# Building the token list of an expert layer: five of six column groups on VectorE instead of every second, and six buffers instead of four

## The reference, cut to what matters

```python
x = x + mamba(layernorm(x), ...)
x = x + ffn(layernorm(x), ...)
# inside ffn, after attention; N = 16384 tokens, 8 experts, top 2, cap = 5120
probs = softmax(h @ router_weight)
top_p, top_i = top_k(probs, 2);  top_p = top_p / sum(top_p)
order = argsort(top_i.reshape(-1))            # choices, expert by expert
within = place of a choice in its expert;  keep = within < cap
padded_ids[slot of the choice] = its token;  padded_probs likewise
out = (gelu(tokens @ w1[e]) @ w2[e]) * padded_probs
moe = zeros.at[padded_ids].add(out)
```

## Time and profile before

| what | value |
|---|---|
| median of three executions | 6568.46 us |
| profiled execution, its own time | 6567.08 us |
| its span, first to last instruction | 6565.4 us |
| busy over the span | PE 93%, POOL 79%, DVE 64%, ACT 54% |
| stretch of the token list (first `hot_lane` to last matmul) | 4440.65 to 4610.45 us of the span |
| expert stage behind it | from 4616 us to the end |

### The profile page before, as it was taken

One profiled execution on the slowest core, in us unless ns is written; L12 is line 12 of the kernel. 1 busy time (PEld: TensorE's weight loads), 2 busy tenths in 40 slices (PEclk: granted clock), 3 DMA queues, 4 the chain that ended last, 5 costly groups with the idle time before them and its releaser, 6 DMA issues. The chain is left out here.

```text
span 6565.4 us, 78602 instructions
## 1 busy us (share of the span) xinstructions
PE 6120.1 (93%) x25316; PEld 3921.9 (60%) x25316; DVE 4215.0 (64%) x5430; ACT 3554.0 (54%) x6449; POOL 5192.8 (79%) x3956
## 2 busy tenths in 40 slices
PE   7999999999999999999998799965899999999999
PEld 3444444444444444444443688854788888888887
DVE  6999999999999999999999377774000000000000
ACT  6677676767776767676766588742222222222221
POOL 6999999999999999999999677739555555545454
PEclk9999999999999999999999999987999999999999
DMA  3555555555555555555555244340566666666554
GB/s 125 164 162 170 166 170 163 167 168 168 163 170 164 172 163 166 167 165 168 164 166 162 67 119 124 113 112 1 178 187 183 187 183 186 184 184 184 176 169 125
DMA packets 564794, 1029.82 MB, mean 157 GB/s; under 512 B 90722, under 2 KB 259172, under 8 KB 529824
## 3 DMA queue, kind: packets, MB, share of 16 engines
q1 hardware_dynamic: 457280, 669.05, 33.2%
q0 software_dynamic: 107104, 355.74, 18.2%
HBM read 926.31 MB, written 88.60 MB: 155 GB/s over the span
## 5 line engine op out<-in xcount | busy, mean ns | idle before, releaser
L365 POOL TENSOR_TENSOR m_dbu<-m_du,m_bb 128x1024 f32<-128x1024 f32 x1024 | 2394.3, 2371 | 0.0
L743 PE MATMUL m_y_bank<-m_prod,m_ident 128*128 128x512 f32 x4096 | 1977.2, 612 | 145.1 <-POOL m_prod L374 145.1
L516 ACT ACTIVATE m_decay<-m_delta,m_a_neg 128x512 f32<-128x512 f32 x2048 | 1419.8, 695 | 726.9 <-DVE m_h L626 724.9
L743 PEld LDWEIGHTS m_y_bank<-m_prod,m_ident 128*128 128x128 f32 x4096 | 789.4, 196 | 1124.5 <-issue 907.9
L626 DVE TENSOR_TENSOR_SCAN m_h<-m_decay,m_h_end,m_dbu 128x512 f32<-128x512 f32 x1024 | 1258.4, 1265 | 3.4 <-ACT m_decay L516 2.5
L1763 DVE TENSOR_SCALAR e_ye<-e_ybank,e_share 128x256 f32<-128x256 f32 x270 | 118.2, 479 | 1768.3 <-PE e_ybank L1796 1768.3
L626 DVE TENSOR_TENSOR_SCAN m_h<-m_decay,m_dbu 128x512 f32<-128x512 f32 x1024 | 1196.2, 1204 | 12.3 <-ACT m_decay L516 11.8
L1744 ACT ACTIVATE e_a<-e_ubank 128x512 f32<-128x512 f32 x540 | 322.4, 597 | 1473.8 <-PE e_ubank L1787 1473.8
L374 POOL TENSOR_TENSOR m_prod<-m_h,m_cb 128x1024 f32<-128x1024 f32 x416 | 985.9, 2370 | 20.4 <-issue 14.6
L1787 PE MATMUL e_ubank<-e_xT,s_w 128*128 128x256 f32 x4320 | 978.4, 380 | 1.3 <-ACT e_xT L1735 1.3
L1796 PE MATMUL e_ybank<-s_w,e_a 128*128 128x256 f32 x4320 | 954.5, 379 | 0.7 <-ACT e_a L1744 0.7
(11 more groups left out here) (211 smaller groups left out, 6683.8 us busy)
## 6 DMA issues: line engine op xcount, KB each, us to landing
m_bb<-rows_bc SPq DMA_DIRECT2D x1024, 256.0 KB, 3.8
m_cv<-rows_bc SPq DMA_DIRECT2D x608, 256.0 KB, 4.0
m_cb<-rows_bc SPq DMA_DIRECT2D x416, 256.0 KB, 3.4
m_xin<-in_x SPq DMA_DIRECT2D x32, 512.0 KB, 5.6
m_xres<-in_x SPq DMA_DIRECT2D x32, 512.0 KB, 5.4
x<-m_xres SPq DMA_DIRECT2D x32, 512.0 KB, 6.2
a_xa<-x SPq DMA_DIRECT2D x64, 256.0 KB, 2.9
a_xr<-x SPq DMA_DIRECT2D x64, 256.0 KB, 3.1
```

Source lines behind the costliest of these rows:

```text
L365: nc.gpsimd.tensor_tensor(dbu[:, slot], du[:, q[1], p * PC:(p + 1) * PC], bb[:, slot].unsqueeze(1).to_broadcast([P, PC, T]), ALU.mult).the ...
L516: nc.scalar.activation(decay[:, cc], delta[:, r, c], ACT.Exp, scale=a_neg[:, c, n:n + 1]).then_inc(decay_done, 1)
L743: ins = nc.tensor.matmul(y_bank[:, cc], ident[:], prod[:, slot, cc], start=False, stop=(n == NS - 1))
```

## The change

`BY_POOL` becomes every fifth group: 4, 9, 14, 19, 24 and 29, six groups in place of sixteen. VectorE makes the hot columns of 26 groups in place of 16. The ring of `hot_lane`, `hot_row` and `hot_column` has six buffers, so every wait on `placed` in the list reaches back six groups instead of four. Since `BY_POOL[-2]` is now group 24, the weights of block 0 are issued behind group 24 and no longer behind group 29, and those of block 1 behind group 29 and no longer behind 31.

```diff
@@ -1396,8 +1396,8 @@
     SPAN = 4
     EACH = SPAN * TOPK
     GROUPS = TILES // SPAN
-    HOT_RING = 4
-    BY_POOL = [g for g in range(GROUPS) if g % 2]
+    HOT_RING = 6
+    BY_POOL = [g for g in range(GROUPS) if g % 5 == 4]
     BY_VECTOR = [g for g in range(GROUPS) if g not in BY_POOL]
     WEIGHTS_AT = 4
     NOWHERE = float(4 * P * COLS)
```

## The result

Four runs of the changed kernel have a median of 6475.7 us (6474.5 to 6479.4), against 6568.2 us before: a ratio of 0.986 (95% interval 0.9843 to 0.9878), 92 us less. The forecast was 6483 us, with a range of 6474 to 6495. In the profiled execution (6479.42 us, span 6477.6) the difference is 87.8 us of span, and the list alone accounts for 88.6: it takes 81.2 us in place of 169.8. The stretch behind it, from the list's last matmul to the first transpose of the expert stage, is 9.9 us after 10.6, and the rest 1944.6 after 1944.3. Where the list starts differs from profile to profile by some us (4438.0 to 4444.8 us over all that follow; 4440.65 before), for reasons ahead of the change. So I compare lengths of the list, and times only beside them.

What follows compares the result with a forecast made beforehand. GpSimd's column groups were taken to bound the list: from 4467.9, groups 14, 19, 24 and 29 at 11.7 us, weights 2.6 and 7.7 end it at 4525.2, 85.2 us earlier: 6481.9, median 6483 us, range 6474 to 6495.

Steps and rivals of the forecast that it cites:

- The bound: Token list: GpSimd's 16 groups of about 10.3 us set its end; time off the list comes off the kernel.
- lower end of the range: Whole kernel: with GpSimd at 9.4 us a group VectorE bounds the list, giving 6476; the range starts at 6474.
- GpSimd's groups: GpSimd's columns in the list: 11.7 us a group beside a busy VectorE, with ends 9.4 and 12.8.
- VectorE's sum: VectorE in the list: 26 x 2.6 + 6 x 0.6 + 3.9 = 75.1 us.
- fulfilled waits: VectorE's already fulfilled waits on `placed`, from group 6 on: taken as nothing, at most 2.6 us in all.
- TensorE's clock: Rival, list: short gaps keep the clock low and TensorE bounds; about 6517 us, chance 0.04.
- the ring's share: List: four buffers instead of six would make each cycle 15.5 us, some 15 us more over four cycles.
- groups 0 to 3: TensorE at the list's start: two groups at the low clock, two at the high, ending at about 4453.9.
- TensorE's wait for group 29: End of the list: TensorE ends group 28 at 4511.9 and waits 5.5 us for GpSimd's group 29.
- Weights and tail: List's end: block 0's two weight DMAs 2.6 us, last three groups 7.7; VectorE's tail and the gather unchanged.
- The rule against the change: The skill's exclusive port lock between VectorE and GpSimd: if it held for columns, moving them to VectorE would stall them.
- VectorE held by GpSimd: Rival, list: 48 GpSimd columns of 1.19 us each hold VectorE, adding 57 us; about 6533 us, chance 0.04.

Runs made afterwards that it cites:

- the split alone: The changed kernel with HOT_RING back from six to four, GpSimd keeping every fifth group: median 6508.9 us, list 111.3 us.

## Why the prediction was right, and where it was not

**The bound.** Right: GpSimd's chain made the list, and the 88.6 us off the list came off the kernel (87.8 us of span). That the ring does nothing without the split was not in the prediction; the run shows it.

**The number.** The median came out 7 us below the forecast and near the lower end of the range, for two reasons. In the profiled execution the forecast was 6481.9 and the time 6479.42, 2.5 us less; the list was shorter by 3.4 (below). The rest is scatter: the prediction set the median 1.4 us above the profiled execution, and it lies 3.7 us below it. The lower end of the range supposed that GpSimd's groups take 9.4 us, which they don't.

**VectorE's sum.** 75.1 us forecast; from the first lane (4441.96) to the last column (4516.24) it was 74.3, with no sign of a price for fulfilled waits. Group 8 was placed 27.3 us into the list, as forecast. But what the sum meant was misread. Of its 2.6 us a group 0.4 is GpSimd's doing, and with no column on GpSimd the same stretch for all 32 groups is 74.3 us as well (4444.76 to 4519.06 in the first such profile). GpSimd's 48 columns took 48 x 0.20 us off VectorE and cost it 48 x 0.20.

**TensorE's clock.** As forecast it rose early, 2.8 us after the first matmul, and stayed at 2.4 GHz, through gaps of up to 0.64 us between groups and one of 3.5 us behind group 4; that rival fell. After the 2.9 us ahead of group 29 it was low, though this pause is shorter than the 3.5 us through which it stayed high: the length of the pause alone doesn't decide it. The window of the change, from 4447.6 until the first matmul of group 29:
```profile
4447.60:4515.70 68.10, 55.92 (x453) 52.07 (x451) 67.93 (x226) 33.98 (x30) 61.91 (x47) 1.00 0.09 32
```
I missed two things about four buffers: that group 4 would wait as well, and that the clock would fall in the waits of 5.2 us in every cycle. 15 us were named for the ring's share, 30 were measured. One sum of the prediction is also off by half a us: by its own terms groups 0 to 3 (two at 3.6 us, two at 1.87, from 4443.5) end at 4454.4 and not 4453.9. It entered nothing, since GpSimd's group 9 had time to spare.

**GpSimd's groups.** The term that was mis-sized: 11.7 us forecast, 10.8 to 10.9 measured. Over the four groups in the chain this makes 3.2 of the 3.4 us by which the list was shorter than forecast; TensorE's wait for group 29 was 2.9 us, not 5.5, and for groups 14, 19 and 24 it waited 0.15 to 0.5 us, not 1 to 2. With 10.9 in place of 11.7 the sum ends at 4467.9 + 4 x 10.9 + 2.6 + 7.7 = 4521.8, 88.6 us earlier than before, as measured.

The loss isn't 0.44 us for every lane. A column that starts while a lane runs waits for its end. A lane that starts over 0.5 us into a column delays it no more and isn't delayed, and one that starts 0.2 us into it waits itself. The three cases in this order, in the trace of the change:
```profile
4489.38 0.68 DVE L1633 TENSOR_TENSOR r_hot_lane<-r_lane_h,r_lane_of_h 128x1024 bf16<-128x1024 bf16 x1
4489.47 1.70 POOL L1470 TENSOR_SCALAR r_hot_column<-r_column_h,r_column_of 128x270 bf16<-128x270 bf16 x1
...
4485.52 1.24 POOL L1470 TENSOR_SCALAR r_hot_column<-r_column_h,r_column_of 128x270 bf16<-128x270 bf16 x1
4486.26 0.68 DVE L1633 TENSOR_TENSOR r_hot_lane<-r_lane_h,r_lane_of_h 128x1024 bf16<-128x1024 bf16 x1
...
4477.39 1.27 POOL L1470 TENSOR_SCALAR r_hot_column<-r_column_h,r_column_of 128x270 bf16<-128x270 bf16 x1
4477.59 0.89 DVE L1633 TENSOR_TENSOR r_hot_lane<-r_lane_h,r_lane_of_h 128x1024 bf16<-128x1024 bf16 x1
```
When the lane starts within 0.1 us after the column, either can be the one that waits: in the change the column did in both such cases, and in the kernel before the lane did in four of five (0.95 to 0.99 us, beside columns of 1.19 or 1.20).


**Weights and tail.** 2.6 us for the two DMAs forecast, 2.7 measured; 7.7 for the last three groups, 7.4 measured. The gather landed in 2.8 us as before.

**The rule against the change.** I put VectorE held by GpSimd at 57 us and a chance of 0.04, since no VectorE column was as long as one of GpSimd's. The direction of that rival was right and its size was not: 0.20 us for each of the 48 columns, about 10 us, where it had 57. These 10 us were already in the 2.6 us a group, which was read beside a busy GpSimd, so the sum came out although its mechanism was misread. The median duration is the same with and without GpSimd (282 and 284 ns), so it could not show the effect; the distance from lane to lane does. The Trainium skill (SBUF — State Buffer, "Who interferes with whom") says that VectorE instructions with two SBUF inputs contend with GpSimd instructions that read, and not with those that only write. The traces agree: GpSimd's columns wait for such lanes, and memsets come every 0.27 us beside them, the shortest distance seen. The same section says that whoever issues first keeps the shared ports for its whole instruction when VectorE is in a two-port mode. No run tells which mode the columns are in; a hold for the whole of a GpSimd column, 1.19 us, is not what they show.

**What the change is worth.** Of the 88.6 us the split alone gives 58.5, and the ring 30.1 more, but only behind the split. The best kernels are those that leave GpSimd no column or hide its chain: 76.5 to 77.2 us, and no column at all is the simplest (6470.8 us against 6477.2 in the same comparison). VectorE sets the end in all three. No run has all columns on VectorE with the ring of four, so whether that kernel needs the larger ring stays open.

## What to carry to other kernels

Before work is split between VectorE and GpSimd, measure the price that the one's instructions put on the other, from start to start and not by the median duration: here a GpSimd column took as much from VectorE as it spared it. Where an engine takes every n-th group of an ordered stream, it must not have to wait for its own last group to be placed, or each cycle adds the placements that it waits for. Here, with every fifth group, that took a ring of six. And a wait for buffers that follows the pace of a slow producer is no reason for more buffers.

## What the runs showed of the hardware

- A GpSimd `tensor_scalar` (1.19 us alone) beside VectorE's busy columns takes 1.24 to 1.42 us, and up to 1.81 in the change if it starts while a VectorE `tensor_tensor` of 0.68 us with two SBUF inputs runs; with one of the inputs in PSUM at most 1.38.
- Such a `tensor_tensor` that starts 0.2 us into the GpSimd instruction takes 0.89 us instead of 0.68; one that starts over 0.5 us into it takes 0.68 and doesn't lengthen the other.
- The GpSimd `tensor_scalar` takes 0.20 us from a VectorE that writes columns; a GpSimd memset of that size about 0.01. The memset itself comes every 0.43 us beside such columns and every 0.27 beside a VectorE `tensor_tensor`.
- A VectorE comparison of 128 x 1024 bf16 takes 0.69 us with bf16 operands in SBUF, and 1.2 us with an fp32 operand in PSUM.
